# Rotary sums of three tiles on VectorE, a block's rows one tile later, and the last attention tile transposed into the score banks

## The reference

```python
x = x + retention_net(layernorm(x))     # 2 layers of retention and a SiLU FFN
x = x + ternary_ffn(layernorm(x))
x = x + local_attention(layernorm(x))
x = x + ternary_ffn(layernorm(x))

# a retention layer, 8 heads of 32
Xn = layernorm(X) * ln1_w + ln1_b
Q, K, V = Xn @ WQ, Xn @ WK, Xn @ WV
Q = Q * cosq + rotate_every_two(Q) * sinq
K = K * cosk + rotate_every_two(K) * sink
Y = groupnorm(((Q @ K.T) * decay_mask) @ V)
Y = (silu(Xn @ WG) * Y) @ WO + X
X = silu(layernorm2(Y) @ w1 + b1) @ w2 + b2 + Y

# local attention, 16 query heads and 4 key heads of 16, window of 64
q, k = rms_norm(x @ Wq.T), rms_norm(x @ Wk.T)      # then rotary, gain, scale
att = softmax(where(causal and distance < 64, q @ k.T, min))
out = pair_mix(att @ v) @ Wo.T
```

## Time and profile before

| | |
|---|---|
| median of 3 runs | 1488.9 us (1485.52 to 1489.1) |
| the profiled execution | 1490.09 us, its span 1488.2 us |
| TensorE busy | 1432.0 us, 96% |
| VectorE busy | 1038.2 us, 70% |
| ScalarE busy | 929.3 us, 62% |
| GpSimd busy | 810.6 us, 54% |
| granted TensorE clock | 0.99 over the run |
| DMA | 26.27 MB, 18 GB/s on average |

### The profile page before, as it was taken

How to read it: one execution, slowest core, us unless ns; L and a number is a source line. 1 busy time by engine, 2 the same in 40 slices (tenths; PEclk the granted TensorE clock), 3 DMA queues, 4 the chain that set the end, 5 groups by cost and what they waited for, 6 DMA issues and landing times. The chain is left out here.

```text
span 1488.2 us, 36345 instructions
## 1 busy us (share of the span) xinstructions
PE 1432.0 (96%) x13066; PEld 1183.5 (80%) x13066; DVE 1038.2 (70%) x2285; ACT 929.3 (62%) x1748; POOL 810.6 (54%) x884
## 2 busy tenths in 40 slices
PE   6999999999998999999999999998999999989998
PEld 4777878888986788888899988886777777758886
DVE  6878877564536887785755668775777777856775
ACT  4665565565543555555655567775777777758775
POOL 2666766312203676663734357775666666636674
PEclk9999999999999999999999999999999999999999
DMA  7000000100001000000300010000000000000111
GB/s 252 2 2 1 0 2 2 36 1 1 1 1 58 2 2 0 1 2 1 128 30 15 1 40 2 0 1 2 2 1 0 0 0 0 1 1 1 38 34 43
DMA packets 21176, 26.27 MB, mean 18 GB/s; under 512 B 1985, under 2 KB 19137, under 8 KB 20929
## 3 DMA queue, kind: packets, MB, share of 16 engines
q1 hardware_dynamic: 20768, 24.61, 5.0%
q10 hardware_dynamic: 288, 0.07, 0.0%
HBM read 20.48 MB, written 4.19 MB: 17 GB/s over the span
## 5 line engine op out<-in xcount | busy, mean ns | idle before, releaser
L548 DVE TENSOR_TENSOR ffn_h_lo<-ffn_h,ffn_h_hi 128x512 fp32r<-128x512 f32 x112 | 86.3, 771 | 122.1 <-ACT ffn_h_hi L759 122.0
L758 ACT ACTIVATE ffn_h<-ffn_hp,c_b 128x512 f32<-128x512 f32 x112 | 77.2, 689 | 145.5 <-PE ffn_hp L857 145.0
L548 DVE TENSOR_TENSOR ternary_ffn_h_lo<-ternary_ffn_h,ternary_ffn_h_hi 128x512 fp32r<-128x512 f32 x128 | 110.9, 866 | 75.8 <-ACT ternary_ffn_h_hi L759 75.5
L2195 POOL TENSOR_TENSOR win_rms<-win_sq_sum,win_minus_half 128x20 f32<-128x20 f32 x31 | 113.2, 3650 | 76.7 <-DVE win_sq_sum L2305 76.7
L1253 POOL TENSOR_TENSOR ret_qk<-ret_qk,ret_qk_sin 128x512 f32<-128x512 f32 x64 | 82.7, 1291 | 105.6 <-DVE ret_qk_sin L1360 105.2
L870 PE MATMUL ternary_ffn_yp<-down_ternary,ternary_ffn_h_hi 128*128 128x256 f32 x512 | 132.0, 291 | 0.0
L870 PE MATMUL ffn_yp<-down_hi,ffn_h_hi 128*128 128x256 f32 x448 | 127.4, 284 | 0.0
L870 PE MATMUL ternary_ffn_yp<-down_ternary,ternary_ffn_h_lo 128*128 128x256 f32 x512 | 127.4, 282 | 0.0
L1259 POOL TENSOR_TENSOR ret_rstd<-ret_sums,ret_minus_half 128x16 f32<-128x16 f32 x32 | 103.6, 3238 | 42.8 <-DVE ret_sums L1402 42.8
L870 PE MATMUL ffn_yp<-down_hi,ffn_h_lo 128*128 128x256 f32 x448 | 124.9, 279 | 0.0
L870 PE MATMUL ffn_yp<-down_lo,ffn_h_hi 128*128 128x256 f32 x448 | 124.9, 279 | 0.0
(11 more groups left out here) (321 smaller groups left out, 4676.4 us busy)
## 6 DMA issues: line engine op xcount, KB each, us to landing
staging<-in_w SPq DMA_DIRECT2D x4, 1024.0 KB, 7.1
ffn_x_in<-in_x SPq DMA_DIRECT2D x8, 512.0 KB, 3.8
X<-in_x SPq DMA_DIRECT2D x7, 512.0 KB, 8.0
out<-X SPq DMA_DIRECT2D x7, 512.0 KB, 2.9
staging<-in_wqkv SPq DMA_DIRECT2D x2, 768.0 KB, 5.4
rotary<-in_rotary SPq DMA_DIRECT2D x1, 1024.0 KB, 6.9
staging<-in_w_up SPq DMA_DIRECT2D x1, 1024.0 KB, 4.9
staging<-in_w_down SPq DMA_DIRECT2D x1, 1024.0 KB, 7.5
```

The source lines that it names most:

```text
L548: nc.vector.tensor_tensor(h_lo[:, m % R, :], h[:, m % R, :], h_hi[:, m % R, :].bitcast(F32), ALU.subtract).then_inc(h_ready, 1)
L758: nc.scalar.activation(h[:, m % R, :], hp[m % 2][:, :], fn, bias=bias)
L2195: nc.gpsimd.tensor_tensor(rms[:, 1, :], sq_sum[:, :], minus_half[:, :], ALU.pow).then_inc(rms_work, 1)
```

## The change

Retention, both layers. Tiles 1, 3 and 5 have their rotary sum on VectorE, right behind `rotate`, and there `values` of tile n comes ahead of `masked` of tile n-1. GpSimd's `scale_in_place(1)` comes one tile later. `input_low` of block 1, its `inputs` on ScalarE, and `own_low(4)` move from the tiles 0 and 1 into tile 2, behind what they stood ahead of.

Local attention. The four groups of the last tile are transposed into the four score banks, in the round of their scores, without waiting for copies. VectorE copies group 1, ScalarE the others. The next stage's first transposes go into `tp`, the second into score bank 1. The last two rounds of TensorE are written in a new order. The statistics, the scales and `next_normalise` come a round earlier, and GpSimd's `even_keys` of the last tile ahead of `values`.

```diff
@@ -1140,6 +1140,10 @@
...
+        def summed_at_once(n):
+            return isinstance(n, int) and n in (1, 3, 5)
         def transposed(b, j):
@@ -1271,7 +1275,7 @@
...
                     n = U * i + k - AHEAD
-                    if live(n, NT):
+                    if live(n, NT) and not summed_at_once(n):
                         rotary_sum(n, k)
@@ -1281,8 +1285,8 @@
...
                         first_scale(1)
-                        if first is not None:
-                            scale_in_place(1)
+                    if at_start(n - 1) and first is not None:
+                        scale_in_place(1)
                     if isinstance(i, int) and i == N and k == U - 1:
@@ -1360,6 +1364,13 @@
...
                 last.then_inc(qk_read, 1)
+            def rotary_sum(n, at):
+                dve.wait_ge(qk_read, n + 1)
+                r = at % 2
+                nc.vector.tensor_tensor(qk[:, r, :, :, :], qk[:, r, :, :, :], qk_sin[:, r, :, :, :], ALU.add
+                                        ).then_inc(qk_done, 1)
@@ -1489,18 +1500,23 @@
...
                         dve.wait_ge(tables_loaded, 16 * (len(first["tables"]) - 2))
+                    if summed_at_once(n):
+                        rotary_sum(n, k - AHEAD)
+                        values(n, k)
                     if live(n - 1, NT):
                         masked(n - 1, k - 1)
-                    if live(n, NT):
+                    if live(n, NT) and not summed_at_once(n):
                         values(n, k)
...
                         aggregate(1, 1)
+                    if at_start(n - 1):
+                        first_normalise(1)
+                    if at_start(n - 2):
+                        input_low(1, 0, 1)
                         if first is not None:
                             own_low(4)
-                    if at_start(n - 1):
-                        first_normalise(1)
                     if k % 2 == 0:
@@ -1510,7 +1526,7 @@
...
                         at = (k - AHEAD) // TB + 1
-                        if fresh(2 * i + at):
+                        if fresh(2 * i + at) and not at_start(n - 1):
                             input_low(2 * i + at, k % TB // 2, at)
@@ -1674,6 +1690,8 @@
...
                         columns_out(n - 2, k - 2)
+                    if at_start(n - 2):
+                        inputs(1, 0, 1)
                     q = 4 * i + (k - AHEAD - 3) // 2
@@ -1708,8 +1726,6 @@
...
                         heads_out(n, k)
-                    if at_start(n - 1):
-                        inputs(1, 0, 1)
                     if at_start(i) and k == TB - 1 and first is not None:
@@ -2120,6 +2136,18 @@
...
+        def final_tile(n):
+            return isinstance(n, int) and n == NT - 1
+        def next_bank(j):
+            return sc[:, 1, :] if j else tp[:, :]
+        def probs_bank(n, g):
+            return sc[:, g, :] if final_tile(n) else tp[:, :]
         def slot(at):
@@ -2210,15 +2238,17 @@
...
                     n = U * i + k
+                    if final_tile(n - 3):
+                        even_keys(n - 3, k - 3)
                     if live(n - 4, NT) and not made(n - 4, 2):
                         values(n - 4, k - 4)
-                    if live(n - 3, NT):
+                    if live(n - 3, NT) and not final_tile(n - 3):
                         even_keys(n - 3, k - 3)
...
                         norm_scale(n, k)
-                    if isinstance(n, int) and n == NT + 2:
+                    if isinstance(n, int) and n == NT + 1:
                         next_scales()
@@ -2259,7 +2289,7 @@
...
                 dve.wait_ge(next_hi_done, j + 1)
-                nc.vector.tensor_tensor(lane_lo[:, 0, j, :], sc[:, j, :], lane_hi[:, 0, j, :].bitcast(F32), ALU.subtract)
+                nc.vector.tensor_tensor(lane_lo[:, 0, j, :], next_bank(j), lane_hi[:, 0, j, :].bitcast(F32), ALU.subtract)
@@ -2337,6 +2367,12 @@
...
+            def probs_copy(n, g):
+                dve.wait_ge(pt_full, WKV * n + g + 1)
+                dve.wait_ge(y_full, n)
+                nc.vector.tensor_copy(pt[:, g, :, :].rearrange("p c n -> p (c n)"), probs_bank(n, g)).then_inc(pt_done, 1)
             def output_low(n):
@@ -2352,7 +2388,7 @@
...
                     n = U * i + k
-                    if live(n - 6, NT):
+                    if live(n - 6, NT) and not final_tile(n - 5):
                         divide(n - 6, k - 6)
@@ -2374,18 +2410,19 @@
...
                         next_input_low(1)
+                    if final_tile(n - 4):
+                        probs_copy(n - 4, 1)
+                        divide(n - 5, k - 5)
                     if live(n - 6, NT):
...
                     if isinstance(n, int) and n == NT:
-                        next_statistics(range(0, 3))
+                        next_statistics(range(0, 5))
                     if isinstance(n, int) and n == NT + 1:
-                        next_statistics(range(3, 6))
+                        next_statistics(range(5, 2 * TB))
+                        next_aggregate()
                     if isinstance(n, int) and n == NT + 2:
-                        next_statistics(range(6, 2 * TB))
-                        next_aggregate()
-                    if isinstance(n, int) and n == NT + 3:
                         next_normalise()
@@ -2416,7 +2453,8 @@
...
                 at_least(act, y_full, n)
-                nc.scalar.activation(pt[:, g, :, :].rearrange("p c n -> p (c n)"), tp[:, :], ACT.Copy).then_inc(pt_done, 1)
+                nc.scalar.activation(pt[:, g, :, :].rearrange("p c n -> p (c n)"), probs_bank(n, g), ACT.Copy
+                                     ).then_inc(pt_done, 1)
@@ -2448,20 +2486,20 @@
...
                 act.wait_ge(qkv_full, NT)
-                nc.scalar.activation(lane_hi[:, 0, j, :], sc[:, j, :], ACT.Copy).then_inc(next_hi_done, 1)
+                nc.scalar.activation(lane_hi[:, 0, j, :], next_bank(j), ACT.Copy).then_inc(next_hi_done, 1)
...
                         input_high(n - 2, k - 2)
-                    if live(n - 5, NT):
+                    if live(n - 5, NT) and not final_tile(n - 5):
                         probs_out(n - 5, 1)
...
                         queries_out(n - 3, k - 3)
-                    if live(n - 5, NT):
+                    if live(n - 5, NT) and not final_tile(n - 5):
                         probs_out(n - 5, 3)
@@ -2479,6 +2517,9 @@
...
                         probs_out(n - 4, 0)
+                    if final_tile(n - 4):
+                        probs_out(n - 4, 2)
+                        probs_out(n - 4, 3)
                     if isinstance(n, int) and n == NT + 4:
@@ -2501,9 +2542,9 @@
...
                 pe.wait_ge(next_xn_done, 1)
-                pe.wait_ge(exp_done, WKV * NT)
+                pe.wait_ge(pt_done, WKV * (NT - 1 + j))
                 for t in range(TB):
-                    last = nc.tensor.transpose(sc[:, j, t * P:(t + 1) * P], next_xn[:, t, j * P:(j + 1) * P], ident[:, :])
+                    last = nc.tensor.transpose(next_bank(j)[:, t * P:(t + 1) * P], next_xn[:, t, j * P:(j + 1) * P], ident[:, :])
                 last.then_inc(next_tp_full, 1)
@@ -2593,9 +2634,10 @@
...
                 pe.wait_ge(exp_done, WKV * n + g + 1)
-                at_least(pe, pt_done, WKV * n + g)
+                if not final_tile(n):
+                    at_least(pe, pt_done, WKV * n + g)
                 for s in range(NC * PAIRS):
-                    last = nc.tensor.transpose(tp[:, s * P:(s + 1) * P], pr[:, g, s, :], ident[:, :])
+                    last = nc.tensor.transpose(probs_bank(n, g)[:, s * P:(s + 1) * P], pr[:, g, s, :], ident[:, :])
                 last.then_inc(pt_full, 1)
@@ -2647,6 +2689,13 @@
...
                     here, past, six = (live(n - lag, NT) for lag in (4, 5, 6))
+                    if final_tile(n - 5):
+                        next_transposes(0)
+                        weighted(n - 5, k - 5)
+                        out_product(n - 6)
+                        transpose_back(n - 5)
+                        next_transposes(1)
+                        continue
                     if here:
@@ -2679,6 +2728,15 @@
...
                         lower(n - 4, 3)
+                    if final_tile(n - 4):
+                        transpose_probs(n - 4, 0)
+                        transpose_probs(n - 4, 1)
+                        transpose_back(n - 5)
+                        transpose_probs(n - 4, 2)
+                        transpose_probs(n - 4, 3)
+                        out_product(n - 6)
+                        transpose_outputs(n - 5)
+                        continue
                     if six:
@@ -2687,9 +2745,6 @@
...
                         transposes(n - 1, k - 1)
-                    if isinstance(n, int) and n == NT + 4:
-                        next_transposes(0)
-                        next_transposes(1)
```

## The result

The changed kernel takes **1485.0 us** (median of 17 runs, 1483.7 to 1487.9) against 1488.6 us (17 runs, 1485.4 to 1489.4) of the kernel before: ratio 0.9981, 95% interval 0.9974 to 0.9989. That is 2.8 us less by the ratio, and 3.6 by the medians. The forecast was 4.9 less, 1484.0; the range of 1480 to 1488 holds it. It lies within the 0.3% that the prediction drew as its bound, while the prediction gave most of its chance to the other side of it.

The account below looks back on a forecast made before the run. TensorE was taken to bound the kernel, with time to gain only in its waits and low clock. Retention -0.3 -0.3 -0.2 and attention's end -4.1 made -4.9 from 1488.9: 1484.0 us, range 1480.0 to 1488.0.

Parts of the forecast that it names:

- Part 1: Retention tiles 3 and 5: VectorE's sum starts transposes 0.62 us sooner but delays `chunk_out`; 0.26 lost a tile, +0.52 a layer.
- Parts 2 and 3: Retention, moved steps and the sums' loss together: -0.29 us in layer 0, -0.30 in layer 1, and 0.1 each for tile 2.
- The size of a fall: Retention: a fall of TensorE's clock to the 1.2 GHz level costs 1.55 us.
- The number of falls: Tiles 1 and 3, both layers: one clock fall in four places 38%, none 30% (1482.5 us), two or more 15% (1485.6 or 1487.1).
- Part 4: SyncE's two 1 MB transfers, issued near 33 us instead of 21.28, land near 41 with 5 us to spare: no cost.
- Part 5: End of local attention: the last tile's transposes no longer wait for copies; -4.1 us.
- About 1.3 of it is clock: End of local attention: about 1.3 us of the 4.1 gained comes from TensorE's clock no longer falling among the last groups.
- the tail behind stays: Behind the last output transposes of local attention: the remaining time is unchanged, with no cost counted.
- Rival 3: Retention: GpSimd holds the six VectorE sums, up to 1.81 us each, giving 1489.9 to 1494.9 us; 7%.
- Rival 4: End of attention: late `even_keys` or another wait replaces the stalls, half of 4.1 us lost, 1486.0 to 1488; 10%.

Follow-up runs that it names:

- e4: Changed kernel with the six rotary sums back on GpSimd and VectorE's earlier order, other moves kept: 1482.6 us, ratio 0.9954 to the kernel before.
- e3: Changed kernel with `masked` ahead of `values` behind VectorE's sum in tiles 1, 3 and 5: 1483.0 us, ratio 0.9957 to the kernel before.
- e5: Changed kernel with useless TensorE transposes filling its waits in tiles 1, 3 and 5: 1483.6 us, ratio 0.9965 to the kernel before.
- e1: Only the retention part of the change, over the attention of the kernel before: 1489.1 us, ratio 0.9999 to the kernel before.
- e6: Changed kernel with the six sums back on GpSimd and useless transposes at the end of attention: 1479.8 us, ratio 0.9943 to the kernel before.
- e8: The kernel before, unchanged, run again for a second profile: 1489.3 us, ratio 1.0005 to the kernel before.
- e12: The changed kernel, unchanged, run again for a second profile: 1485.4 us, ratio 0.9977 to the kernel before.
- e11: Changed kernel, sums split between VectorE and GpSimd, `masked` before `values`, useless transposes before rotary transposes and at attention's end: 1481.0 us, ratio 0.9949 to the kernel before.
- e9: The kernel before with 7 useless transposes ahead of attention's last output product and 6 behind it: 1487.3 us, ratio 0.9994 to the kernel before.
- e10: Attention part alone over the old retention, with 3, 7 and 6 useless transposes at attention's end: 1485.0 us, ratio 0.9977 to the kernel before.

## Why the prediction was right, and where it wasn't

**Part 1, the sum on VectorE: right.** All six sums took 693 ns, the transposes came 0.6 us sooner, and the loss was 0.27 a tile where 0.26 stood. The new wait of `chunk_out` is there six times. The prediction's own sum booked the six sums as a loss. e4 and e3 show that this was the lever: with the sums left on GpSimd, or with `masked` first, a layer is 0.9 us shorter.

**Parts 2 and 3, the moved steps: right.** R of layer 0 went from 34.13 to 32.17 with one fall of 1.55 less: -0.41, against -0.29 and -0.1. R of layer 1 without a fall (e5) is 0.51 under before's 32.59, against -0.30 and -0.1. The scores wait for nothing.

**The size of a fall: right.** 1.55 was read off the difference of two stretches; layer 1 of e5 against that of after gives 1.54.

**The number of falls: the step that failed.** The prediction took one fall left in the four places as the likeliest, with 30% for none and 15% for two or more. Three profiles of this retention have one, two and two. One fall was also what before had, so each further one is a loss against before: 1.67 - 1 = 0.67 falls, by 1.5, is 1.0 us, and it eats the 0.9 of parts 1 to 3. That fits the 0.9999 of e1, whose interval is wider than either term. That the first profile of after had just the one fall forecast was chance. The prediction had seen the danger ("the new idle time is 0.6 + 0.8 = 1.4 a tile, between that 1.23 and the 2.10") and had then weighed it by the total alone. The single wait of 1.23 was followed by a fall in none of 15 places in five profiles of the old retention, and in none of 8 in e4 and e6.

**Part 4, the later prefetch: right.** It is issued at 32.19 and ScalarE's split at 46.26 waits for nothing.

**Part 5, the end of attention: right to its edge, and wrong behind it.** A shrank by 4.1 us from profile to profile. "About 1.3 of it is clock" was right too, 4.1 - 2.75, where the clock falls there; it did in three of four profiles with the old end. But "the tail behind stays" wasn't: F is 5.39 to 5.41 in three profiles with the old end and 5.24 to 6.66, on average 6.1, in seven with the new one, against 4.48 without a fall. So 0.7 us went back there on average over these kernels. The two profiles of the changed kernel itself have the lowest of the seven, 5.24, so for it alone no profile shows this term. The prediction's sum ended at the stage's edge and priced no fall behind it.

With these two terms the sum is -0.9 + 1.0 - 4.1 + 0.7 = -3.3, between the 2.8 of the ratio and the 3.6 of the medians. It was made after the result, from few profiles, and is no proof of its terms. One check from all runs bears out that the clock took part of the gain: the mean granted clock is 0.9916 in the 25 runs of after and after again, 0.9928 in the 74 of before. Times the span that is 12.5 us of (1 - clock) against 10.7; the 1.8 more are worth 0.8 to 1.4 us by the estimates under e8 and e12. Where they lie, these numbers don't say.

**The rivals.** Rival 3, sums held by GpSimd, didn't come, and its 1.81 us was not the price of a gated product: that product had itself been held, and takes 1.27 where nothing is ahead of it (last section). The sums were not held because GpSimd had only short steps there, and it was GpSimd that waited (0.56 us for the scale step at 22.09, where e11 has 0.20 at 24.39 beside none of VectorE's sums). Rival 4 came for a small part, at another place than it named.

## What to carry to other kernels

A wait that is taken from TensorE's path is worth what its successor leaves: ask which work is queued behind the moved instruction, and put the one that TensorE needs first at the head (here `masked` ahead of `values`, or the sum left where it was). Count the clock as a term of its own at every place where idle times come close together, behind the edge of the changed stage as well, and take several profiles before its falls are counted. Useless transposes in a free bank are a cheap test of it: in the tiles they took 1.4 us off by the medians (2.4 by the ratios), at the end of attention 2.8 (1.6) in e6, but in e9 and e10 nothing beyond the intervals.

## What the runs showed of the hardware beside that

**Two engines, one access.** Tile 5 of layer 0 in after, VectorE's low half of a block row beside GpSimd's gated product, answers to the earlier trace rows:

```profile
51.99 1.27 POOL L1272 TENSOR_TENSOR ret_yt<-ret_yt,ret_gate 128x512 f32<-128x512 f32 x1 [2.07 <-ACT ret_yt L1633]
...
52.36 1.45 DVE L1350 TENSOR_TENSOR xt_lo<-xt,xt_hi 128x512 fp32r<-128x512 f32 x1
```

The same subtraction takes 0.68 us at 38.81 in e4. There it starts 0.01 us ahead of a scale step of GpSimd, and the small step is held; the last row is that step in after, with no instruction of VectorE beside it:

```profile
38.81 0.68 DVE L1350 TENSOR_TENSOR xt_lo<-xt,xt_hi 128x512 fp32r<-128x512 f32 x1
38.82 0.73 POOL L1202 TENSOR_SCALAR ret_scale_work<-mean_var 128x4 f32<-128x4 f32 x1
```

```profile
34.61 0.19 POOL L1202 TENSOR_SCALAR ret_scale_work<-mean_var 128x4 f32<-128x4 f32 x1
```

So in these rows an instruction of either engine with two operands in SBUF held the other engine's that came later, until about its own end: 52.36 + 1.45 is 0.55 behind the end of GpSimd's product, for a subtraction of 0.68. That fits too. In before that subtraction ran on VectorE from 54.58, and the gated product, which started at the same 54.58, took 1.81 instead of 1.27; then VectorE's product at 55.50 was held until 56.48, where GpSimd's ended at 56.39:

```profile
54.58 0.68 DVE L1346 TENSOR_TENSOR xt_lo<-xt,xt_hi 128x512 fp32r<-128x512 f32 x1
```

The Trainium skill, GPSIMD Engine Reference, section Specifications, names contention with VectorE instructions that have two SBUF inputs; these rows agree, and add that the one that starts first loses nothing.

**Idle times in pieces.** In three profiles of this retention 0.6 to 0.7 and 0.8 to 0.9 us of idle time, with 0.65 us of transposes between them, were followed by a fall in 5 of 12 places; 0.6 to 0.7 and 0.5 to 0.6 (e3) in none of 4; one of 1.23 in none of 23.
